# Final edge rows of a two-layer graph kernel made by GpSimd inside the second node pass, from o kept in SBUF, with the list of nodes filled from its end

## The reference, cut to what matters

```python
edge_index = jnp.stack([src, dst])
h = jnp.maximum(_layernorm(x, axis=-1), 0.0)
x = x + _L0_gnn_ref(src, dst, h, L0_gnn_W, L0_gnn_b)      # degree-scaled graph convolution
h = jnp.maximum(_layernorm(x, axis=-1), 0.0)
x = x + _L1_gnn_ref(h, edge_index, edge_attr_4, edge_attr_16, ...)
# the end of _L1_gnn_ref: every node has o = B @ WB + h @ Wsc; B is zero where no edge arrives
mu = jnp.mean(o0, 0); var = jnp.mean((o0 - mu) ** 2, 0)
n0 = (o0 - mu) * rsqrt(var + eps) * gamma0 + beta0
nrm1 = jnp.mean(jnp.sum(o1 * o1, -1) / 3.0, 0)
n1 = o1 * (rsqrt(nrm1 + eps) * gamma1)[None, :, None]
return jnp.concatenate([n0, n1.reshape(n, 3 * C)], -1)
```

## Time and profile before

| | |
|---|---|
| median of 3 runs | 2157.86 us (2145.46 to 2160.13) |
| the profiled execution's own time | 2154.57 us |
| span of the profile, first to last instruction | 2152.7 us |
| mean granted TensorE clock | 0.931 |
| busy share of PE, DVE, ACT, POOL | 79%, 83%, 71%, 51% |
| p2 from the statistics' end to the last sum | 1641 to 2004 us |
| f, POOL's indirect DMAs | 2008 to 2143 us |

### The profile page before, as it was taken

One profiled execution on the slowest core, in us unless ns is written; L12 is line 12 of the kernel. 1 busy time (PEld: TensorE's weight loads), 2 busy tenths in 40 slices (PEclk: granted clock), 3 DMA queues, 4 the chain that ended last, 5 costly groups with the idle time before them and its releaser, 6 DMA issues.

```text
span 2152.7 us, 53890 instructions
## 1 busy us (share of the span) xinstructions
PE 1692.0 (79%) x14246; PEld 1444.6 (67%) x14344; DVE 1780.1 (83%) x7827; ACT 1529.4 (71%) x3485; POOL 1095.4 (51%) x1065
## 2 busy tenths in 40 slices
PE   5979999999999798888578777679997777787100
PEld 3657888888888677777466666568885777777100
DVE  5778999999999688888488888779987999999664
ACT  3757788878788577877566666579996999999100
POOL 3105654455545577787567777744430222122576
PEclk9989999999999899999798999989998999999655
DMA  4689666666666577777456666567785888888784
GB/s 143 239 202 217 239 235 232 230 241 244 232 234 210 148 157 160 164 158 156 78 106 120 122 119 118 102 205 248 246 218 189 290 287 291 287 288 288 261 279 148
DMA packets 206640, 437.75 MB, mean 203 GB/s; under 512 B 49624, under 2 KB 87900, under 8 KB 206570
## 3 DMA queue, kind: packets, MB, share of 16 engines
q1 hardware_dynamic: 137018, 361.19, 49.2%
q0 software_dynamic: 56448, 74.95, 19.1%
q10 hardware_dynamic: 13104, 0.81, 1.5%
HBM read 220.18 MB, written 219.18 MB: 204 GB/s over the span
## 4 chain that ended last, share of the span: by engine, by line
PE 37%; issue 15%; ACT 13%; DMA 12%; POOL 10%; DVE 9%; SPq 1%; DVEq 1%; ACTq 0%; POOLq 0%
PE bank L817 15%; ACT hb L1087 7%; PE bank L797 6%; POOL big L503 4%; DMA big<-x_tab,idx 3%; DVE st L1349 2%; POOL msg_tab L514 2%; PE bank L776 2%; POOL x_tab L514 2%; DMA big<-in_x_dram,idx 2%; DMA out_dram<-osb,idx 2%; ACT ht L1236 2%; PE bank L813 2%; PE bank L938 2%; PE bank L948 2%
## 5 line engine op out<-in xcount | busy, mean ns | idle before, releaser
L1349 DVE BATCH_NORM_STATS2 st<-big 128x6 f32<-128x256 f32 x882 | 314.9, 413 | 87.8 <-DMA big<-x_tab,idx 65.4
L817 PE MATMUL bank<-w_sb,ht 128*128 128x256 f32 x1568 | 371.6, 380 | 9.8 <-issue 7.7
L817 PEld LDWEIGHTS bank<-w_sb,ht 128*128 128x128 f32 x1568 | 299.9, 191 | 47.5
L797 PE MATMUL bank<-ident,hb 128*128 128x128 f32 x1568 | 211.1, 278 | 89.6 <-ACT hb L1087 75.7
L503 POOL DMA_INDIRECT big<-x_tab,idx x196 | 193.1, 985 | 144.4 <-issue 51.9
L469 POOL DMA_INDIRECT node_edge<-node_tab,idx x196 | 188.3, 961 | 138.9 <-issue 50.6
L797 PEld LDWEIGHTS bank<-ident,hb 128*128 128x128 f32 x1568 | 178.3, 142 | 119.2 <-issue 83.6
L563 POOL TENSOR_TENSOR big<-big,bias 128x256 f32<-128x256 f32 x98 | 72.0, 734 | 324.1 <-ACT hb L1087 285.4
L1048 ACT ACTIVATE hb<-big,rs 128x256 f32<-128x256 f32 x392 | 207.5, 590 | 21.1 <-DVE rs L1372 21.1
L1087 ACT ACTIVATE hb<-big,rs 128x256 f32<-128x256 f32 x392 | 213.5, 591 | 4.0 <-DVE rs L1372 3.9
L1031 ACT ACTIVATE sd<-mv,eps_col 128x4 f32<-128x4 f32 (+1 forms) x343 | 103.2, 301 | 154.1 <-DVE mv L1358 153.8
(11 more groups left out here) (248 smaller groups left out, 4360.2 us busy)
## 6 DMA issues: line engine op xcount, KB each, us to landing
big<-in_x_dram SPq DMA_DIRECT2D x97, 512.0 KB, 4.2
x_tab<-x1b SPq DMA_DIRECT2D x97, 512.0 KB, 2.9
big<-x_tab SPq DMA_DIRECT2D x97, 512.0 KB, 4.2
out_dram<-x1b SPq DMA_DIRECT2D x97, 512.0 KB, 2.9
x_odd<-x1b SPq DMA_DIRECT2D x48, 512.0 KB
big<-x_odd SPq DMA_DIRECT2D x48, 512.0 KB
msg_tab<-zeros SPq DMA_DIRECT2D x50, 256.0 KB, 2.2
tpw_tab<-tpb SPq DMA_DIRECT2D x49, 256.0 KB, 2.0
```

What stands on the lines that cost most here:

```text
L797: last = nc.tensor.transpose(bank[q][:, (2 * j + k) * P:(2 * j + k + 1) * P], hb[:, s.slot(2, 2), 2 * q + j, k * P:(k + 1) * P], ident[:])
L817: last = mm(y, ht[:, q, (2 * j + k) * P:(2 * j + k + 1) * P], w_sb[:, k, :], start=False, stop=(j == 1 and k == 1))
L1349: last = v.bn_stats(st[:, k, j, :], row)
```

## The change

In words, with the names of the diff:

- `o_rows` holds o of all 49 steps in SBUF (`[P, S, 2, D]`, 98 KB a partition). To make room, most tiles of the earlier stages are laid into the same memory (`under`); ACT's squares go to a tile of their own (`squares`), ACT's copy of o goes into `o_rows`. `edge_o`, its 49 stores and its 49 loads go.
- `rows_step` on POOL, 49 steps at the place of POOL's p2 loop: four tensor_tensor instructions make the final row in `o_rows` from o, `scale`, x1 and `bias`. x1 comes by SP's `f_load` (256 KB), now issued inside p2 at SP's steps 8 to 56, behind the load of group k and ahead of the store of group k-6; it waits for the rows of four steps before (four slots of `f_x`).
- `bias` of p2 moves from POOL to PE: one more bf16 matmul for each half group (line 1019 of the changed kernel), with `bias` split into three bf16 parts by ten small DVE instructions behind the statistics; PE waits for them (`fs["bias3"]`).
- The list is filled from its end: PE counts the nodes behind, DVE computes `EDGES - 1 - rank`. The nodes still go upwards with the places, but the empty places come first, and the last step holds the highest nodes.
- `thr`: between e2 and e3 DVE and PE work out, for each of the 49 steps, the last node group that it writes (`stores_first`). SP counts p2 stores that have landed (`f["stored"]`), two steps behind their issue. In `f_step` POOL loads the number of its step from SBUF into a register and waits for that many stores, instead of for all 98.
- DVE's f stage goes.

```diff
+            def rows_step(s):
+                one = Chain(pool, f["scaled"], 1, s.at())
+                landed(pool, f_in, s)
+                x1, o, scaled = f_x[:, s.slot(0, 4)], o_rows[:, s.k], squares[:, s.slot(0, 2)]
+                g.tensor_tensor(x1[:, :, 0:C], x1[:, :, 0:C], bias[:].unsqueeze(1).to_broadcast([P, 2, C]), ALU.add)
+                one(g.tensor_tensor(scaled, o, scale[:].rearrange("p k c -> p (k c)").unsqueeze(1).to_broadcast([P, 2, D]),
+                                    ALU.mult))
+                g.tensor_tensor(o[:, :, 0:C], scaled[:, :, 0:C], x1[:, :, 0:C], ALU.add)
+                by_channel = [rows[:, :, C:D].rearrange("p i (x c) -> p i c x", x=3) for rows in (scaled, x1)]
+                g.tensor_tensor(o[:, :, C:D].rearrange("p i (c x) -> p i c x", x=3), by_channel[0], by_channel[1],
+                                ALU.add).then_inc(f["rows"].sem, 1)
+            run_written_out(S, 0, rows_step)
...
             def f_step(s):
-                done(pool, f["rows"], s, 0)
-                if s.k == 0:
-                    all_landed(pool, y_out, G)
+                n = pool.value_load(stores_first[0:1, s.k:s.k + 1], min_val=1, max_val=G)
+                pool.wait_ge(f["stored"].sem, n)
+                settle(pool)
...
-                if s.live(4):
-                    done(sp, e3["o"], s, 4)
-                    sp.dma_start(edge_o[s.at(4)].rearrange("p (a d) -> p a d", a=2),
-                                 osb[:, s.slot(4, 2), :, D:2 * D]).then_inc(eo_out[s.slot(4, 2)].sem, 16)
...
-                if s.k == G:
-                    all_landed(sp, eo_out, S)
-                    for k in range(4):
-                        f_load(Step(0, k, k, S, 4))
+                if XS <= s.k < XS + S:
+                    f_load(Step((s.k - XS) // 4, (s.k - XS) % 4, s.k - XS, S, 4))
                 if s.live(6):
                     done(sp, p2["out"], s, 6, per=2)
...
+                if s.live(8):
+                    landed(sp, y_out, s, 8)
+                    sp.sem_inc(f["stored"].sem, 1)
...
                         pe.wait_ge(p2["ht"].sem, s.at(3) * 2 + q + 1)
+                        mm(bank[2 + q][:].rearrange("p (j d) -> p j d", j=2)[:, :, 0:P], ones_bf[:],
+                           bias3[:].rearrange("p j d -> p (j d)"), start=True, stop=False)
...
-                    landed(act, eo_out, s, 7)
                     o = o_bank[a][:].rearrange("p (k i c) -> p i k c", k=4, i=2)
-                    s_act(osb[:, a, :, 0:D].rearrange("p i (k c) -> p i k c", k=4), o, ACT.Square)
-                    nc.scalar.copy(osb[:, a, :, D:2 * D].rearrange("p i (k c) -> p i k c", k=4), o
+                    s_act(squares[:, a].rearrange("p i (k c) -> p i k c", k=4), o, ACT.Square)
+                    nc.scalar.copy(o_flat[:, bass.ds(s.at(5) * (2 * D), 2 * D)].rearrange("p (i k c) -> p i k c", i=2,
...
-            v.tensor_scalar(of_node[:, :, 2], bank[5][:, 0:G * J], float(T), None, ALU.mult)
-            link(v.tensor_copy(rank_hi[:], bank[5][:, 0:G * J]))
+            link(v.tensor_scalar(of_node[:, :, 2], bank[5][:, 0:G * J], -1.0, float(EDGES - 1), ALU.mult, ALU.add))
+            link(v.tensor_copy(rank_hi[:], of_node[:, :, 2]))
+            v.tensor_scalar(of_node[:, :, 2], of_node[:, :, 2], float(T), None, ALU.mult)
...
+                dve.wait_ge(fs["weights"].sem, 1)
+                part = Chain(dve, fs["bias_chain"])
+                part(v.tensor_copy(bias_f[:, 0, :], bias[0:3, :]))
+                part(three_parts(part, bias_f, bias_bf, bias3[0:3, 0, 0:C]))
+                v.tensor_copy(bias3[0:3, 1, 0:C], bias3[0:3, 0, 0:C]).then_inc(fs["bias3"].sem, 1)
...
-                    done(dve, p2["biased"], s, 3)
```

More of the change, by code:

```diff
@@ L36 @@
 assert TAIL == TAILP * J and 0 < LASTP < T
+assert NG == 1 << 9 and (N + 2 * P) // NG >= G
 class Step:
@@ L245, in build @@
         x1b = sb("x1b", [P, 2, J * D])
-        h2b = sb("h2b", [P, 2, J, ROW])
+        h2b = under([P, 2, J, ROW])
         st = sb("st", [P, 2, J, 6])
@@ L290, in build @@
         a_bank, o_bank = (bank[2], bank[3]), (bank[6], bank[5])
-        f_o, f_x = eq, addb
-        f_rows = [osb[:, a // 2, a % 2, :].rearrange("p (i d) -> p i d", i=2) for a in range(4)]
         def xj(t, slot, width):
@@ L376, in build @@
         y_in, y_out = reused(odd_in, S, 4) + used[4:], sems("y_out", 2)
-        f = named("f", "chain rows")
-        f_in, f_out = reused(msg_got, S, 4), sems("f_out", 4)
+        f = named("f", "scaled rows stored")
+        f_in, f_out = reused(msg_got, S, 4), sems("f_out", 1)
+        thr = named("thr", "chain spread of_step row first")
         for chain, per in (("chain_a", 1), ("chain_b", 1), ("chain_c", 3)):
@@ L910, in _ @@
             run(pe, S, 4, e2_step)
+            pe.wait_ge(thr["chain"].sem, 5)
+            mm(bank[5][0:S, 0:P], last_group[:], ident[:], start=True, stop=True).then_inc(thr["spread"].sem, 1)
+            pe.wait_ge(thr["of_step"].sem, 2)
+            mm(bank[5][0:1, 0:S], last_of_step[:, 1:2], ident[0:S, 0:S], start=True, stop=True
+               ).then_inc(thr["row"].sem, 1)
             pe.wait_ge(e2["add"].sem, e2["add"].base + S)
@@ L1720, in _ @@
             run_groups(dve, 3, p2_step)
-            all_landed(dve, eo_out, S)
-            def f_step(s):
-                if s.live():
-                    a = s.slot(0, 4)
-                    one = Chain(dve, f["chain"], 2, s.at())
-                    landed(dve, f_in, s, 0, dmas=2)
-                    o, x1, result = f_o[:, a], f_x[:, a], f_rows[a]
-                    one.mark(v.tensor_tensor(o, o, scale[:].rearrange("p k c -> p (k c)").unsqueeze(1)
-                                             .to_broadcast([P, 2, D]), ALU.mult))
-                    landed(dve, f_out, s, 4, dmas=2)
-                    v.tensor_tensor(x1[:, :, 0:C], x1[:, :, 0:C], bias[:].unsqueeze(1).to_broadcast([P, 2, C]), ALU.add)
-                    one.wait()
-                    for i in range(2):
-                        last = v.tensor_tensor(result[:, i, C:D].rearrange("p (c x) -> p c x", x=3),
-                                               o[:, i, C:D].rearrange("p (x c) -> p c x", x=3),
-                                               x1[:, i, C:D].rearrange("p (x c) -> p c x", x=3), ALU.add)
-                    one(last)
-                    v.tensor_tensor(result[:, :, 0:C], o[:, :, 0:C], x1[:, :, 0:C], ALU.add).then_inc(f["rows"].sem, 1)
-                    one.end()
-            run(dve, S, 0, f_step)
 _INS = ["x", "src", "dst", "edge_attr_16", "edge_attr_4", "L0_gnn_W", "L0_gnn_b", "L1_gnn_W_up0", "L1_gnn_W_up1",
```

198 lines of the change are left out of this document (118 added, 80 removed).

## The result

The changed kernel takes 2045.1 us in the median of 4 runs (2034.4 to 2046.1), against 2156.8 us (2145.5 to 2160.1) for the kernel before: a ratio of 0.948, 95% interval 0.946 to 0.951. The forecast was 2049, from 2024 to 2092. The profiled execution took 2046.1 us, its span is 2043.9.

What follows compares the result with a forecast made beforehand. DVE was taken to set p2's pace, PE and ACT to fill e3, and f to be a serial POOL tail; 2154.6 - 132.3 - 2.9 + 20 + 5 + 2 + 2 + 1 = 2049.4 us, range 2024 to 2092.

Steps and rivals of the forecast that it cites:

- The tail, -132.3: In f: scatters go under p2, only the last step waits for the last store; 132.3 us less.
- POOL on time, 15 us early: In p2: after the rows, 48 scatter steps take 152 us, 46 remaining groups 167; register load 0.6 us each.
- A block at 3.6 us: POOL's rows step in p2: 1152 elements at 2.87 ns, 3.30 us, plus 0.3 waiting for its own result.
- POOL beside DVE, +20: In p2: POOL's adds hold DVE's product with two SBUF inputs, 0.4 us a group for 49 groups; 20 us more.
- DMA, +5, and the stall, -2.9: In p2: late stores from fuller DMA, 5 us more; DVE's one store wait at p2's end goes, 2.9 less.
- Behind the statistics, +2: Early in p2: ten small dependent DVE instructions for the bias take 2.5 us, partly covered; 2 us more.
- PE in p2, 0: Two bias matmuls a group on PE, 0.4 us, mostly covered: 0, up to 10 us if not.
- e3, +2: In e3: stores and ACT's wait go, two small matmuls a step come, same columns in all; 2 us more.
- Setup, +1: In setup: POOL's extra constants lie before DVE's start; 1 us more.
- POOL is the pace: Rival, 22%: in p2, POOL's blocks take 4.7 us or register loads over 1 us; 2075 to 2105 us.
- No collision: Rival, 20%: in p2, POOL's and DVE's phases miss each other and DMA has room; about 2023 to 2032 us.
- The gate isn't early: Fourth rival, 4%: stored count late or SP's waits hold p2, little of the tail moves; 2135 to 2157 us.

Runs made afterwards that it cites:

- late_gate: The changed kernel with one more wait on POOL, for all 98 stored groups, ahead of the first scatter: 2171.7 us, ratio 1.010.
- contig: The changed kernel with the last add of a rows step walking straight through its rows in input and output: 2038.9 us, ratio 0.947.
- no_rows: The changed kernel without POOL's four instructions of each rows step; f_x loads, semaphores and scatters stay: 2031.5 us, ratio 0.945.
- psum_mean: The changed kernel with bn_aggr's results of p2 from group 3 on in a free PSUM bank: 2033.5 us, ratio 0.947.
- no_bias3: The changed kernel without the group rows' bias: no bias chain on DVE, no wait for it, no bias matmuls on PE: 2043.0 us, ratio 0.949.
- bias_pool: The changed kernel with the group rows' bias back on POOL, all adds ahead of the first scatter, without PE's bias matmuls: 2193.9 us, ratio 1.019.

## Why the prediction was right

The time, 2049 against 2045, is right, and the mechanism that carries it, the early gate, is shown; but two terms were off in opposite directions, POOL beside DVE by 8.5 us too much and e3 by 4 too little. That the sum came within 4 us is luck in part also because e3's start, which no edit touches, lies anywhere in 20 us. In the order of the prediction's steps:

- **The tail, -132.3:** measured -131.3 from group 97 to the end. The last scatter stands 2.2 us behind the last store's landing, within the 3 us named. late_gate shows that it is the gate that does it. How much of it needs the list filled from its end was not run.
- **POOL on time, 15 us early:** right in kind, wrong in size. The rows' part was near (3.73 us a block against 3.6). The register load was taken as 0.6 us and shows nothing: POOL's gap between two DMAs is 0.30 us with it and without. 0.6 x 48 = 29 us, which with the 15 expected make 44, and POOL waited 46.4 us for the gate. None of it is on the path. Only ahead of the first scatter, where no DMA runs before it, do 1.77 us pass behind the last add; whether the load is in them isn't shown.
- **A block at 3.6 us:** 3.73. 2.87 ns an element was a poor price, since it left no room for a fixed part: 128 elements take 455 ns and 512 take 1278, so 2.14 ns an element and 0.18 us a piece. By that 1152 elements in four pieces are 3.19 us, plus the walk by channel, which the forecast had at nothing and contig at 0.54: 3.73. The wait for POOL's own result, taken as 0.3, shows as 3.8 us in 49 blocks, 0.08 each. The errors cancelled.
- **POOL beside DVE, +20:** the term that was mis-sized: 11.5 us, 0.24 us a group and not 0.4. The product's time above 155 ns adds up to 11.0 us of it, and no_rows and psum_mean, where that excess is gone, run at the old pace: it is the lock. The formula had DVE wait through the first two instructions of a block, up to the gap before the third. Where it waits, it waits for the last add, since POOL hardly ever stands idle between blocks: 49 blocks run from 1671.08 to 1861.09, 3.88 us apart, p2's own period (3.89). I read this as DVE being pulled along by POOL's cycle, each product waiting until the block is over; that contig's shorter block halves the wait fits, but the phase itself was not tested.
- **DMA, +5, and the stall, -2.9:** together +2.1, measured +1.9 from group 51 to 97 in this profile and nothing before. Both parts are there: DVE waits 5.0 us for landings, and the one wait of 2.9 us is gone (the longest is 0.8). Three more profiles of the same p2 give +3.2, +4.8 and +4.8 and 7.0 to 8.7 us of such waits, so the closeness of 2.1 and 1.9 is partly luck. The full rate by proportion, 343 GB/s, was too low: p2 ran at 361 and 363 GB/s in no_rows and psum_mean with no time lost.
- **Behind the statistics, +2:** 2.5, and about 2 by no_bias3.
- **PE in p2, 0:** no_bias3 and psum_mean show no cost.
- **e3, +2:** the other step that failed: +6.0. The argument was "with the same columns in all", and columns don't add up where rows 0, 32, 64 and 96 run beside each other; the added o sums both went to the part that was already full. The sums grew by 0.18 us a step, 8.9 in all, of which e3 shows 6.0. I had named a period longer by over 0.1 us as a sign of being wrong, and it is: 6.0/49 = 0.12 on average, and 4.28 to 4.47 from one step's sums to the next in the median.
- **Setup, +1:** +0.7 in the pair of profiles, which can't be told from the 20 us by which e3's start differs among runs.

Of the rivals, "POOL is the pace" didn't come about, and bias_pool shows what it would have been: at 4.65 us a group the 48 periods take 48 us more than before, by the path that the forecast gave, SP's load and the store behind it. 43.7 us of the 48 are DVE's waits for landings. The forecast took a lead of 14 us off for such a pace; the run shows none, and why isn't known. "No collision" didn't either, though it is what psum_mean makes of the kernel. "The gate isn't early" is late_gate, at 2172 and not at the 2135 to 2157 that I gave it, since it pays p2's losses as well. The chances of the three faster cases add up to 0.92; the 0.93 of the forecast, with a part of the fourth taken off, doesn't follow from them.

## What to carry to other kernels

A serial tail of scatters can go under the stage that it waits for if it is ordered so that the early pieces need little of that stage, and if nothing that waits for the end of the stage stands ahead of them in their engine's queue; here the gate is worth 123 us, more than the whole gain, and moving the work without it gains nothing. Before work goes to POOL beside a full DVE, look for DVE instructions with two SBUF inputs in the same stretch, and put one of the inputs in PSUM (here 12 us). Small matmuls that write to single rows belong spread over the four parts of the array so that none is much fuller in columns than the others (here 8 us).
